# A four-layer graph network on one core: the biases of two products added by GpSimd, and three orders in the count sweeps

## What is computed

```python
# layer 2, the end of it
x1 = layer_norm(x + h, ln1_w, ln1_b)
f = jax.nn.gelu(x1 @ W1 + b1, approximate=False) @ W2 + b2
out = layer_norm(x1 + f, ln2_w, ln2_b)
# layer 3, the end of it
x = _layernorm(h + o, ln1_g, ln1_b)
f = jax.nn.relu(x @ W1 + b1) @ W2 + b2
return _layernorm(x + f, ln2_g, ln2_b)
```

## Time and profile before

| | us |
|---|---|
| median of 3 runs | 529.7 |
| lowest, highest | 529.44, 530.45 |
| profiled execution | 532.03 |
| its span, first to last instruction | 530.1 |
| PE busy in the span | 503.2 |
| DVE, ACT, POOL busy | 382.8, 225.7, 277.7 |

### The profile page before, as it was taken

One profiled execution on the slowest core, in us unless ns is written; L12 is line 12 of the kernel. 1 busy time (PEld: TensorE's weight loads), 2 busy tenths in 40 slices (PEclk: granted clock), 3 DMA queues, 4 the chain that ended last, 5 costly groups with the idle time before them and its releaser, 6 DMA issues.

```text
span 530.1 us, 7860 instructions
## 1 busy us (share of the span) xinstructions
PE 503.2 (95%) x2483; PEld 344.5 (65%) x2498; DVE 382.8 (72%) x972; ACT 225.7 (43%) x474; POOL 277.7 (52%) x283
## 2 busy tenths in 40 slices
PE   7999999999999899999999999999999999899992
PEld 2444444444786564787788888889888786565771
DVE  5999979999986776977654863764348625776586
ACT  2102370004614776557461244435535225776365
POOL 5877777777403989402552544523532752867101
PEclk9999999999999999999999999999999998999998
DMA  6923410000293441050853564322453853100002
GB/s 192 354 74 108 113 28 1 0 0 2 85 355 100 133 122 61 4 176 19 246 155 104 183 187 137 124 80 80 131 172 97 254 163 88 52 0 1 2 0 79
DMA packets 32409, 56.48 MB, mean 107 GB/s; under 512 B 5152, under 2 KB 8686, under 8 KB 31864
## 3 DMA queue, kind: packets, MB, share of 16 engines
q1 hardware_dynamic: 19276, 31.35, 19.1%
q0 software_dynamic: 11728, 18.92, 12.0%
q10 hardware_dynamic: 1372, 5.81, 3.0%
HBM read 51.79 MB, written 4.26 MB: 106 GB/s over the span
## 4 chain that ended last, share of the span: by engine, by line
PE 70%; POOL 9%; DVE 7%; issue 6%; DMA 5%; ACT 4%; POOLq 0%; DVEq 0%; ACTq 0%
PE bank L563 12%; PE bank L564 12%; PE bank L565 12%; PE bank L586 11%; PE bank L692 4%; PE bank L783 3%; PE bank L782 3%; POOL wl L389 3%; PE bank L679 3%; DMA edge_bias<-nbias 3%; POOL sp L403 2%; PE bank L670 2%; PE bank L644 2%; POOL edge_bias L444 1%; DVE sp L1479 1%
## 5 line engine op out<-in xcount | busy, mean ns | idle before, releaser
L389 POOL TENSOR_TENSOR wl<-wraw,wh 128x512 fp32r<-128x512 f32 (+1 forms) x78 | 102.1, 1324 | 71.6 <-DMA wh<-w 15.5
L586 PE MATMUL bank<-hot 128*128 128x512 bf16 x514 | 114.3, 379 | 4.3 <-DVE hot L1303 3.4
L586 PEld LDWEIGHTS bank<-hot 128*128 128x128 bf16 x528 | 51.2, 98 | 67.5 <-DVE hot L1303 6.4
L444 POOL DMA_INDIRECT edge_bias<-ew,cell_at x68 | 71.1, 1046 | 30.3 <-issue 17.7
L563 PE MATMUL bank<-wh,tl 128*128 128x512 f32 x176 | 69.5, 395 | 0.1
L565 PE MATMUL bank<-wh,th 128*128 128x512 f32 x176 | 68.8, 391 | 0.0
L564 PE MATMUL bank<-wl,th 128*128 128x512 f32 x176 | 68.7, 390 | 0.0
L1303 DVE TENSOR_SCALAR hot<-iota,pair_dst,digit 128x1024 bf16<-128x1024 f16 x68 | 41.9, 616 | 0.2 <-issue 0.2
L955 ACT ACTIVATE sp<-sp,peak 128x512 f32<-128x512 f32 x44 | 31.8, 723 | 23.6 <-DVE peak L1479 23.2
L1302 DVE TENSOR_SCALAR hot<-iota,ef 128x512 bf16<-128x512 f16 x68 | 37.7, 554 | 4.9 <-PE bank L586 3.9
L1284 DVE SCALAR_TENSOR_TENSOR eq<-keyb,key,later 128x384 f16<-128x384 f16 (+1 forms) x68 | 40.1, 612 | 0.0
(11 more groups left out here) (239 smaller groups left out, 1062.1 us busy)
## 6 DMA issues: line engine op xcount, KB each, us to landing
wraw<-w SPq DMA_DIRECT2D x26, 256.0 KB
wh<-w POOLq DMA_DIRECT2D x6, 1024.0 KB, 6.3
keyb<-edge_keys ACTq DMA_DIRECT2D x4, 1088.0 KB, 9.7
wh<-w_rel POOLq DMA_DIRECT2D x4, 1024.0 KB, 5.9
wraw<-w_rel SPq DMA_DIRECT2D x16, 256.0 KB
wraw<-w_qkv SPq DMA_DIRECT2D x8, 256.0 KB
wh<-w_o POOLq DMA_DIRECT2D x2, 1024.0 KB, 6.8
count_rows<-counts SPq DMA_DIRECT2D x1, 2048.0 KB, 14.1
```

The source lines that it names most:

```text
L389: pool.tensor_tensor(wl[n % WSLOTS][:, k, 0:width], wraw[:, q % 3, 0:width], wh[n % WSLOTS][:, k, 0:width], ALU.subtract).then_inc(s["w_lo ...
L444: pool.indirect_dma_start(out=bias_dram, out_offset=bass.IndirectOffsetOnAxis(ap=cell_at[:, c:c + 1], axis=0), in_=ew[:, c:c + 1], in_offs ...
L586: mm = pe.matmul(ps(name)[:], hot[:, slot, 0, i * P:(i + 1) * P], hot[:, slot, 1 + kind, :], start=False, stop=last, skip_group_check=True)
```

## The change

Eight bias products leave PE: those of `f2` and `f3`. Their biases are now added to `h` itself by GpSimd, one TENSOR_TENSOR of 128x512 a tile, after the tile's transposes have read it (`wait_full` on `turn2` or `turn4`) and before `centre(5, i)` or `centre(8, i)` reads it; DVE waits for these through a new semaphore `bias_added`. The bias of layer 2 is loaded to all partitions of `par[:, 4, :]` by a DMA that GpSimd issues, that of layer 3 by ACT's DMA, now 128 rows in place of two. DVE's second `bias_rows` goes, one of four masks goes, and SP loads three bias vectors at the start, not four.

The three orders: `iota` is SP's first load instead of ACT's; `second` and `bias_rows` stand behind loop 1 instead of in block 2; and two of the four key comparisons of the block between the sweeps stand after the second build, ahead of the copies.

```diff
--- SP
+            eng.dma_start(iota[:], iota_d.to_broadcast([P, 2 * N])).then_inc(s["ld_iota"], 16)
             eng.dma_start(ei[:], edges.rearrange("a p c -> p a c")).then_inc(s["ld_edge"], 16)
...
-            for n, name in enumerate(("b0_o", "b0_1", "b2_self", "b2_2")):
+            for n, name in enumerate(("b0_o", "b0_1", "b2_self")):
--- GpSimd
-            for n in range(4):
+            for n in range(3):
                 link(pool.tensor_scalar(masks[:, n, :], ident[:], 0.0, None, ALU.mult))
...
+            pool.wait_ge(s["res_ready"], 2 * T)
+            pool.dma_start(par[:, 4, :], rows_of["b2_2"].to_broadcast([P, D])).then_inc(s["ld_b2"], 16)
             cast(13)
-            pool.wait_ge(normed[4], T)
+
+            def biased(t, i, loaded):
+
+                wait_full(pool, (f"turn{t}", i))
+                pool.wait_ge(loaded, 16)
+                pool.tensor_tensor(h[:, i, :], h[:, i, :], par[:, 4, :], ALU.add).then_inc(s["bias_added"], 1)
+
+            for i in range(T):
+                biased(2, i, s["ld_b2"])
             low(13)
...
             next_residual(3, 1)
+            for i in range(T):
+                biased(4, i, s["ld_b3"])
             for i in range(T - 2):
                 normalise(9, i)
--- PE
-                bias(name, 3)
+                begin(name)
...
-            pe.wait_ge(s["add2_ready"], 4)
...
-                bias(("f3", 2 * part), 0)
-                bias(("f3", 2 * part + 1), 0)
--- ACT
-            act.dma_start(iota[:], iota_d.to_broadcast([P, 2 * N])).then_inc(s["ld_iota"], 16)
...
-            act.wait_ge(s["res_ready"], 2 * T)
-            act.dma_start(par[0:2, 4, :], rows_of["b3_2"].to_broadcast([2, D])).then_inc(s["ld_bias"], 16)
+            act.wait_ge(s["bias_added"], T)
+            act.dma_start(par[:, 4, :], rows_of["b3_2"].to_broadcast([P, D])).then_inc(s["ld_b3"], 16)
--- DVE
                 build_chunk(FIRST_PLACED * RING + slot, slot)
-                if slot == 1:
-                    dve.wait_ge(s["ld_ident"], 16)
...
-                if slot == 2:
-                    dve.wait_ge(s["ld_bias"], 64)
-                    bias_rows(rows[:], slice(0, P), 0)
...
+            dve.wait_ge(s["ld_bias"], 48)
+            bias_rows(rows[:], slice(0, P), 0)
             dve.wait_ge(ld_keys[2], 16)
             dve.wait_ge(ld_keys[3], 16)
             for slot in range(RING - 1):
                 dve.wait_ge(s["hot_used1"], before - RING + slot + 1)
                 build_chunk(before + slot, slot)
+                if slot == 1:
+                    mark(behind, 0)
+                    mark(behind, 1)
+                    settle(behind, behind // GROUP, 0)
...
-            dve.wait_ge(s["ld_bias"], 80)
-            wait_full(dve, ("f2", T - 1))
-            bias_rows(par[0:2, 4, :], slice(0, 2), 2)
...
             dve.wait_ge(ld_par[0], 48)
+            dve.wait_ge(s["bias_added"], T + 1)
             centre(8, 0, ("f3", 0), h[:, 0, :])
```

More of the change, by code:

```diff
@@ L195, in build @@
         deg = sb("deg", [P, 6, T], F32)
-        masks = sb("masks", [P, 4, P], F32R)
+        masks = sb("masks", [P, 3, P], F32R)
         wh = [sb(f"wh{s}", [P, K, D], F32R) for s in range(WSLOTS)]
@@ L835, in first_half @@
                 name, cut = ("f2", i), slice(i * P, (i + 1) * P)
-                bias(name, 3)
-                product(name, lambda k: (hidh[:, k, cut], hidl[:, k, cut]), w_tile(13), K, start=False, stop=False,
+                begin(name)
+                product(name, lambda k: (hidh[:, k, cut], hidl[:, k, cut]), w_tile(13), K, stop=False,
                         ready=(lambda k: pe.wait_ge(s["hidl_ready"], k + 1)) if i == 0 else None)
@@ L906, in _ @@
                     w_ready(20)
-                bias(("f3", 2 * part), 0)
-                bias(("f3", 2 * part + 1), 0)
                 for i in (2 * part, 2 * part + 1):
                     name, tile = ("f3", i), slice(i * P, (i + 1) * P)
-                    finish(product(name, lambda k: (hidh[:, k, tile], hidl[:, k, tile]), w_tile(20), 2, start=False,
+                    begin(name)
+                    finish(product(name, lambda k: (hidh[:, k, tile], hidl[:, k, tile]), w_tile(20), 2,
                                    ready=(lambda k: pe.wait_ge(s["hidl_ready"], 8 + i + k + 1)) if i % 2 == 0 else None), name)
@@ L1365, in _ @@
             before, behind = CBLOCKS[0] * RING, (CBLOCKS[0] - FIRST_PLACED) * RING
+            dve.wait_ge(s["ld_ident"], 16)
+            link(dve.tensor_reduce(second[:], ident[:, 1::32], AX_X, ALU.add))
+            link(dve.tensor_scalar(second[:], second[:], -1.0, None, ALU.mult))
+            dve.wait_ge(s["ld_bias"], 48)
+            bias_rows(rows[:], slice(0, P), 0)
             dve.wait_ge(ld_keys[2], 16)
@@ L1374, in _ @@
             build_chunk(before + RING - 1, RING - 1)
-            for k in range(GROUP):
-                mark(behind, k)
-                if k % 2:
-                    settle(behind, behind // GROUP, k // 2)
+            mark(behind, 2)
+            mark(behind, 3)
+            settle(behind, behind // GROUP, 1)
             def rest_of(pair, tile, count):
@@ L1800, in _ @@
             affine_and_add(8, 1)
+            dve.wait_ge(s["bias_added"], T + 3)
             centre(8, 2, ("f3", 2), h[:, 2, :])
             inverse_root(9, 0)
+            dve.wait_ge(s["bias_added"], T + 4)
             centre(8, 3, ("f3", 3), h[:, 3, :])
```

8 lines of the change are left out of this document (4 added, 4 removed).

## The result

| | before | after |
|---|---|---|
| median, first comparison (6 runs each), us | 529.85 | 533.76 |
| lowest, highest | 529.44, 530.45 | 530.73, 536.01 |
| ratio, 95% interval | | 1.0063 (1.0039 to 1.0087) |
| second comparison (29 and 6 runs) | 531.44 | 536.10, ratio 1.0084 (1.0053 to 1.0115) |
| third comparison (20 and 7 runs) | 531.07 | 535.35, ratio 1.0075 (1.0046 to 1.0105) |

The change makes the kernel slower by 3.9 to 4.7 us. The forecast was 530.2, half a microsecond slower than before, with a range of 528.0 to 531.9: the direction came out, the size is some eight times as large and far outside the range. Chips differ by 1 to 2 us, so each kernel is compared only with runs of the kernel before on its own chip.

The account below looks back on a forecast made before the run. The prediction took PE to be the bound, busy 503.2 us of a 530.1 us span. Its terms, -0.4 (sweeps), +0.3 (layer 2) and +0.6 (end), gave +0.5 on the 529.7 median: 530.2 us, range 528.0 to 531.9.

Parts of the forecast that it names:

- Start, +0.45: Kernel start: `iota` issued ahead of `ei` on SP delays `ei`, which DVE waits for, by 0.45 us.
- the two bounds: Kernel start: delay 0 if both loads shared the engines anyway, +1 us if `ei` waits for 256 KB.
- Block 2, wait gone: Sweep 1, chunk 12: PE's wait of 1.24 us disappears, leaving PE 0.8 us ahead of before.
- The border, +0.8: Between the sweeps: work ahead of DVE's four copies makes PE start sweep 2 at 67.1, not 66.33: +0.8 us.
- 1.1 us of lead: Sweep 1: DVE reaches chunk 12 earlier by 1.1 us and keeps that, leaving loop 1 at 59.3, not 60.38.
- rival 4: Border: DVE's lead is lost in block 2 or loop 1; sweep 2 starts 2 us late, 531.4 us total; chance 0.10.
- Sweeps in all, -0.4: Start through both sweeps: PE ends sweep 2 0.4 us earlier than before, and that gain stays.
- bounds of -0.85 and +1.0: Sweeps: -0.85 us if the start loses nothing, +1.0 if DVE's lead doesn't carry.
- Layer 2, +0.75 and -0.91: Layer 2: held DVE rows delay `hid2` by 0.75 us; four dropped products save PE 0.91; together +0.3.
- The end, +0.6: Layer 3: addition 2 holds DVE's affine of tile 3, so `f3` starts later and the end comes 0.6 us later.
- rival 3: Layer 3: DVE's affine of tile 3 starts just ahead of addition 2; +2.0 us there, 531.6 total; chance 0.18.

Follow-up runs that it names:

- a2: Kernel before with only the three orders of the sweeps; all eight bias products stay on TensorE: 532.91 us against 531.44, ratio 1.0036.
- a3: Changed kernel with the three orders undone, both biases still on GpSimd: 532.42 us against 531.44 for the kernel before, ratio 1.0016.
- b3: Changed kernel with idle products filling TensorE's waits at the end, the border and attention 3: 533.37 us against 531.07 for the kernel before, ratio 1.0052.

## Why the prediction was wrong, step by step

- **Start, +0.45: wrong.** `ei` is issued 0.44 later and the cast starts at 4.72, not 4.91; over all traces the first chunk starts at 7.07 on average with this order (twelve) and at 7.23 without it (eight). Of the two bounds, 0 was right: a load in line ahead of `ei` didn't delay its landing.
- **Block 2, wait gone: right.**
- **The border, +0.8: the step that failed first, and the next one hangs on it.** Sweep 2's first chunk was forecast at 67.1. It is at 67.50 to 68.40 in seven traces with the three orders (mean 68.0), 66.33 to 66.76 in eight without (mean 66.5): +1.5. The prediction let DVE carry its 1.1 us of lead to 59.3. It doesn't: DVE leaves loop 1 at 59.7 to 60.6 (once at 58.4, with a held build of 1.8 us still to come), about where it left before the change (60.38). The steps from there to the copies were sized rightly: 5.0 us forecast, 4.9 to 5.0 in these six. The lead going missing was rival 4, given 0.10. Its reason against ("no idle time in loop 1") was read from a DVE that was late; one that is earlier meets the ring, as the slowest trace shows below, where its one wait for PE takes 0.57 us. In the seven traces DVE's idle time between 34 and 47 us comes to 0.6 to 1.2 us. The ring may not be all. In these six, and in the kernel before, a last build of 1.8 to 2.3 us, in place of 0.35 or 0.54, ends 0.15 to 0.3 us behind a GpSimd subtraction, and DVE is out of the loop within 0.7 us of that subtraction's end. The prediction priced held instructions in layers 2 and 3 and not in the sweeps. GpSimd in turn waits for DVE's `cell_at` at times, so which of the two sets that moment isn't shown, and no run separates this from the ring.

```profile
44.62 0.35 DVE L1312 TENSOR_SCALAR hot<-iota,ef 128x512 bf16<-128x512 f16 x1 [0.57 <-PE bank L599]
...
58.23 2.32 DVE L1313 TENSOR_SCALAR hot<-iota,pair_dst,digit 128x1024 bf16<-128x1024 f16 x1
58.97 1.28 POOL L390 TENSOR_TENSOR wl<-wraw,wh 128x512 fp32r<-128x512 f32 x1
```

- **Sweeps in all, -0.4: wrong, and the largest miss among the terms of the sum.** Sweep 2 takes 61.97 to 62.50 us to `q0` with the orders when the clock holds, and 61.97 to 64.19 (mean 62.9) without: half a microsecond won on average, not the 1.2 that the border's +0.8 and the total of -0.4 implied, and nothing between the fastest of either kind. So the sweeps cost 1.4 us at full clock, outside the bounds of -0.85 and +1.0. And at attention 0's first scores the seven traces with the orders stand 1.9 us later on average than the eight without (164.4 and 162.5), 1.4 without the two that dropped at the border. a2 lost 1.5.
- **Layer 2, +0.75 and -0.91: right in mechanism and size, but for the end.** To `hid2` +0.97 on average (eight traces against ten), `hid2` to `v3` -0.85, `v3` to attention 3 +0.4, since `q3` waits for `low(16)` at times:

```profile
420.28 0.50 PE L575 MATMUL bank<-th,wl 128*128 128x512 f32 x1 [0.90 <-POOL wl L389]
```

  That is a3's trace. In sum +0.5; forecast +0.3.
- **The end, +0.6: right.** 25.36 to 25.45 us at full clock in six traces (three of them with filled waits), 24.78 before. It was closer than forecast: addition 2 starts 0.04 us ahead of the affine row, not 0.18; had it come behind, rival 3 would have applied.
- **The clock: not in the sum at all.** The text asked what each wait costs until TensorE goes on, never what TensorE does to its clock meanwhile, though the profile before already had 0.992. Drops came at the border in 2 of 7 traces with the three orders and in none of the others, at the end in 4 of 7 traces that have the wait of 1.95 us unfilled and in none of the others. A drop costs 1.26 us at the end, 0.9 at attention 3, some 1.5 at the border. Under 0.993 were 16 of 19 runs of the changed kernel and 51 of 139 of the kernel before. What the change's lower mean clock (by 0.0056 to 0.0064) costs comes out differently by the way it is reckoned. Within the kernel before, 0.001 of mean clock goes with 0.23 to 0.32 us: 1.3 to 2.0 us. Within the changed kernel's own runs it goes with 0.45 to 0.58 us: 2.5 to 3.7. And one drop of 3.41 us at half clock is 0.0032 of a span of 530, so by an estimate the difference is about two drops more a run, at 1.26 to 1.5 each: 2.2 to 3.0.

Together: border and sweeps at full clock 1.4, layer 2 0.5, layer 3 0.6, in sum 2.5, which fits the 2.3 that b3 kept at the clock of the kernel before. With the clock at 1.3 to 2.0 the sum is 3.8 to 4.5, measured 3.9 to 4.7; with the two other reckonings it is 4.7 to 6.2, too much. So the account closes only by the lowest price of the clock. It is an account from averages over traces with 0.5 us of scatter in several stages. That the border, the held rows and the clock all take part is shown; how the 4 us divide among them isn't. Open are why `q0` to attention 0 takes 33.1 to 34.2 us with the orders and 33.0 to 33.3 without, and what stops DVE near 78 us (3.31 us): it stands there for 0.4 to 3.5 us in 12 of the 20 traces and not at all in the other eight.

The Trainium skill (SBUF — State Buffer, the section on the two separate sides) names DVE instructions in a two-port mode as held too, not only those with two operands in SBUF. The traces fit this: builds of the one-hot rows, which read one tile, take 1.84 us in place of 0.35 where GpSimd's subtraction runs. That the builds run in such a mode no trace shows, and the build below starts 0.39 us before the subtraction, while GpSimd was still issuing a scattering DMA (56.80 to 57.81). The prediction had used only half of that rule.

```profile
57.44 1.84 DVE L1312 TENSOR_SCALAR hot<-iota,ef 128x512 bf16<-128x512 f16 x1
57.83 1.28 POOL L390 TENSOR_TENSOR wl<-wraw,wh 128x512 fp32r<-128x512 f32 x1
```

## What to carry to other kernels

Work taken off the bound engine is not a gain if what replaces it makes that engine wait. A product of 0.23 us inside a wait was free here (nine of them left the last stage at 19.5 us), and the mean clock was higher with them. Before moving work ahead of a hand-over, ask whether the lead that should pay for it can be carried there at all, or whether a ring of four slots cuts it off or another engine's instructions hold it up. And trace the changed kernel more than once where its runs scatter: the first profile here was the fastest of 19 and showed a gain.

## What the runs showed of the hardware

TensorE needn't stand still to lose its clock: 1.98 us busy out of 4.10, or 2.65 out of 4.60, went ahead of a drop to 1.2 GHz. The same wait is followed by a drop in one execution and not in the next: the wait of 1.95 us before tile 3's transposes was followed by one in 4 of 7 traces. So one kernel has several times: the 19 runs of the changed one lie near a mean clock of 0.994, 0.990, 0.987 or 0.984, from 530.7 us at the first to 537.9 at the last, and a change can act on how often each comes. At the start the full clock came anywhere from 4.8 to 11.5 us into the span; of the seven traces with the three orders, the three where it came by 6.1 us have the shortest sweep 1 (56.1 us), the four where it came behind 10 us the longest (56.9 to 57.4).
